# The second cross attention of a two-layer decoder, by half token tiles with folded keys

## The reference

```python
def _L1_xattn_ref(inputs_q, inputs_kv, Wq, Wk, Wv, Wo, bo, gq, gk):
    ...
    q = jnp.einsum('bsd,dhe->bshe', inputs_q, Wq)
    k = jnp.einsum('bsd,dhe->bshe', inputs_kv, Wk)
    v = jnp.einsum('bsd,dhe->bshe', inputs_kv, Wv)
    q = _rmsnorm(q, gq)
    k = _rmsnorm(k, gk)
    head_dim = q.shape[-1]
    scores = jnp.einsum('bqhe,bkhe->bhqk', q, k) / jnp.sqrt(jnp.asarray(head_dim, q.dtype))
    attn = jax.nn.softmax(scores, axis=-1)
    x = jnp.einsum('bhqk,bkhe->bqhe', attn, v)
    out = jnp.einsum('bqhe,hed->bqd', x, Wo) + bo
    return out
```

## Time and profile before

| | us |
|---|---|
| median of three runs | 1205.21 |
| lowest and highest | 1202.03, 1206.45 |
| profiled execution, its own time | 1207.17 |
| its span in the trace | 1205.5 |
| PE busy | 894.1 (74%) |
| DVE busy | 871.1 (72%) |
| ACT busy | 661.3 (55%) |
| POOL busy | 256.1 (21%) |

### The profile page before, as it was taken

One profiled execution on the slowest core, in us unless ns is written; L12 is line 12 of the kernel. 1 busy time (PEld: TensorE's weight loads), 2 busy tenths in 40 slices (PEclk: granted clock), 3 DMA queues, 4 the chain that ended last, 5 costly groups with the idle time before them and its releaser, 6 DMA issues. The chain is left out here.

```text
span 1205.5 us, 12085 instructions
## 1 busy us (share of the span) xinstructions
PE 894.1 (74%) x3656; PEld 499.5 (41%) x3656; DVE 871.1 (72%) x1703; ACT 661.3 (55%) x1829; POOL 256.1 (21%) x153
## 2 busy tenths in 40 slices
PE   2561478998989589898815248599898976898893
PEld 2450335554366334344414124455435643344432
DVE  1268646886389589999716875587846967999993
ACT  1413369992435285785712053999352435686691
POOL 1011106884070100000000200288515201000000
PEclk9865587998979799999957558699997997999997
DMA  8100012330000000000010000133100000000000
GB/s 217 35 0 1 0 40 59 93 94 0 1 1 1 1 0 1 0 1 1 1 50 1 0 1 5 58 97 90 35 1 1 1 1 1 1 0 1 1 0 18
DMA packets 26814, 27.41 MB, mean 23 GB/s; under 512 B 7172, under 2 KB 17146, under 8 KB 26746
## 3 DMA queue, kind: packets, MB, share of 16 engines
q1 hardware_dynamic: 24776, 24.63, 7.2%
q10 hardware_dynamic: 1970, 1.97, 0.6%
...
HBM read 25.28 MB, written 1.31 MB: 22 GB/s over the span
## 5 line engine op out<-in xcount | busy, mean ns | idle before, releaser
L1489 POOL TENSOR_TENSOR rs<-ve,minus_half 128x4 f32<-128x4 f32 (+2 forms) x60 | 101.7, 1702 | 816.0 <-DVE ve L1119 686.8
L877 PE MATMUL ps<-mem,ident 128*128 128x512 f32 x512 | 234.3, 607 | 27.7 <-DVE mem L1457 26.9
L909 ACT ACTIVATE mem<-ps 77x512 f32<-77x512 f32 (+7 forms) x172 | 103.6, 605 | 241.7 <-PE ps L818 61.1
L1079 ACT ACTIVATE mem<-mem 128x32 f32<-128x32 f32 x1024 | 217.8, 312 | 0.0
L1302 DVE TENSOR_TENSOR_SCAN mem<-mem,ps 128x1024 f32<-128x1024 f32 x64 | 146.0, 2285 | 45.2 <-PE ps L722 45.2
L1504 POOL TENSOR_TENSOR mem<-mem 128x1024 f32<-128x1024 f32 x64 | 150.8, 2360 | 116.7 <-DVE mem L1302 116.6
L1457 DVE SCALAR_TENSOR_TENSOR mem<-mem 128x1024 f32<-128x1024 f32 x128 | 159.2, 1279 | 13.3 <-ACT mem L1079 11.8
L877 PEld LDWEIGHTS ps<-mem,ident 128*128 128x128 f32 x512 | 95.3, 192 | 165.7 <-issue 95.3
L729 PE MATMUL ps<-mem,ident 128*128 128x512 f32 x256 | 121.7, 602 | 0.0
L1449 DVE TENSOR_TENSOR mem<-mem 128x1024 f32<-128x1024 f32 x96 | 113.0, 1218 | 0.3
L1008 ACT ACTIVATE mem<-mem 128x256 f32<-128x256 f32 x256 | 105.2, 493 | 0.1
...
## 6 DMA issues: line engine op xcount, KB each, us to landing
...
```

Of the source, the lines that this page charges most:

```text
L877: mm = pe.matmul(ps[:, j, :], ident[:], WH[s][:, h % WB, j * 512:(j + 1) * 512], start=(h == 0), stop=(h == PH - 1), skip_group_check=True)
L909: ins = nc.scalar.activation(to, of, ACT.Copy, **kw)
L1079: ins = nc.scalar.activation(SVA[s][:, n % 2, i * NK:(i + 1) * NK], sims[:, 1, h, :], ACT.Identity, bias=sims[:, 0, h, i:i + 1])
L1489: nc.gpsimd.tensor_tensor(RS[s][0:rows, i * n:(i + 1) * n], VE[s][0:rows, i * n:(i + 1) * n], minus_half[0:rows, 0:n], ALU.pow)\
```

## The change

The fifth sublayer is computed in another arrangement, and part of it moves.

- The keys' part becomes a generator `memory`, merged with the scan's by stage (`merged`): keys and their squares come at stage 5 + NS of the scan, ahead of the scan's output product at 6 + NS. The gains are still folded into the turned keys; the keys are then folded with Wq: `KW` holds for each head a 128 x 77 matrix, made from `a_qT` (Wq turned once in preparation) and the keys, so scores come from x directly. Values times Wo are laid out as ten chunks of 128 rows of the 16 x 77 = 1232 (head, context) pairs (`VW`); the shifted context for a chunk that crosses a head comes from `CTP`, the context with 128 zero columns at either side.
- Queries are only made for their mean squares: tokens on partitions, a tile of 128 tokens by 1024 features in two banks, squared by ScalarE, reduced by VectorE, power by GpSimd, once for each tile.
- The loop runs over eight units u: four token tiles by two halves of eight heads. Scores of a unit are two matmuls of 308 columns into banks 0 and 1. VectorE takes the maximum of each head and multiplies it by minus the root (`NM`). ScalarE reads the scores from PSUM and writes the exponential, one instruction for each head, with `RS` as scale, `NM` as bias and the sum over the row in `SM`. VectorE takes the reciprocal and multiplies the probabilities of the unit (128 x 616).
- The probabilities of a tile are turned in ten chunks, in groups of 4, 4 and 2 (one group after the first half of heads, two after the second), copied by VectorE, and multiplied with `VW`; the result has tokens on the partitions, in bank 3, and the residual reads it there.
- The `BLEND_LANES` branches go; both lanes took them before, so the scan's instructions are the same.

The diff, cut to what is added in these places; lines removed in `cross1` are those described above.

```diff
@@ -84,10 +84,16 @@
-GB = 3
+HC_COLS = H * C
+CK = -(-HC_COLS // P)
+GROUPS = [(0, 4), (4, 8), (8, CK)]
+GROUPS_OF = [GROUPS[0:1], GROUPS[1:3]]
+def chunk_rows(i):
+    return min(P, HC_COLS - i * P)
...
+pe.wait_ge(p_late, ALL_LATE)
+for j in range(HP):
+    mm = pe.transpose(PS[0][:, j // 4, (j % 4) * P:(j % 4 + 1) * P], a_q[:, j * P:(j + 1) * P],
                       ident[:])
...
+def merged(*runs):
+    stage = [next(r, None) for r in runs]
+    while any(n is not None for n in stage):
+        n, i = min((n, i) for i, n in enumerate(stage) if n is not None)
+        yield n
+        stage[i] = next(runs[i], None)
...
+def memory(s):
+    ps = PS[s]
+    yield 5 + NS
+    w.next(G("scan_done", s))
+    for j in range(2):
+        pe.matmul(ps[0:C, 2 + j, :], CTP[s][:, P:P + C], a_k[:, j * 512:(j + 1) * 512],
+                  start=True, stop=True).then_inc(G("k_ready", s), 1)
+    yield 5.9 + NS
+    w.next(G("kn_ready", s))
+    for j in range(HP):
+        mm = pe.transpose(ps[:, 2 + j // 4, (j % 4) * C:(j % 4 + 1) * C],
+                          KN[s][:, 2 * j:2 * j + 2, :].rearrange("p a b -> p (a b)"),
+                          ident[0:C, 0:C])
+    mm.then_inc(G("k_ready", s), 1)
+    for half in range(2):
+        yield 6.2 + 0.2 * half + NS
+        if half == 0:
+            w.next(G("kT_ready", s))
+        else:
+            w.next(G("m_sb", s))
+        for j in range(4 * half, 4 * half + 4):
+            for a in range(2):
+                mm = pe.matmul(ps[:, 2 + a, j % 4 * C:(j % 4 + 1) * C],
+                               a_qT[a * E:(a + 1) * E, j, :], KT[s][a * E:(a + 1) * E, j, :],
+                               start=True, stop=True)
+        mm.then_inc(G("k_ready", s), 1)
+    for n, (c0, c1) in enumerate(GROUPS):
+        yield 6.6 + 0.1 * n + NS
+        if n >= 1:
+            w.next(G("v_sb", s))
+        for i in range(c0, c1):
+            rows = chunk_rows(i)
+            heads = [h for h in range(H) if h * C < i * P + rows and (h + 1) * C > i * P]
+            for h in heads:
+                at = P + i * P - h * C
+                mm = pe.matmul(ps[0:rows, 1, (i - c0) * P:(i - c0 + 1) * P],
+                               CTP[s][:, at:at + rows], a_vo[:, h, :],
+                               start=(h == heads[0]), stop=(h == heads[-1]))
+        mm.then_inc(G("v_ready", s), 1)
+def scan_memory(s):
+    yield from merged(scan(s), memory(s))
...
+for k in range(NB):
+    yield 1 + k
+    if k == 0:
+        w.next(G("xT_ready", s))
+        w.next(G("v_sb", s))
+    elif k == 1:
+        w.next(G("m_sb", s))
+    else:
+        w.next(G("qsq_ready", s))
+    for j in range(2):
+        mm = pe.matmul(ps[:, k % 2 * 2 + j, :], XT[s][:, k * P:(k + 1) * P],
+                       a_q[:, j * 512:(j + 1) * 512], start=True, stop=True)
+    mm.then_inc(G("aq_ready", s), 1)
+def scores(u):
+    k, g = u // 2, u % 2
+    if u == 0:
+        w.next(G("qsq_ready", s), 2)
+    else:
+        w.next(G("p_ready", s))
+    for a in range(2):
+        h = 8 * g + 4 * a
+        mm = pe.matmul(ps[:, a, 0:4 * C], XT[s][:, k * P:(k + 1) * P],
+                       KW[s][:, h:h + 4, :].rearrange("p a b -> p (a b)"), start=True, stop=True)
     mm.then_inc(G("s_ready", s), 1)
+def weights_turned(k, c0, c1):
+    if (c0, c1) in (GROUPS_OF[0][0], GROUPS_OF[1][0]):
         w.next(G("pn_ready", s))
+    if k or c0:
+        pe.wait_ge(G("wT_ready", s), k * len(GROUPS) + GROUPS.index((c0, c1)))
+    p = SC[s][:, k % 2].rearrange("p a b -> p (a b)")
+    for i in range(c0, c1):
+        rows = chunk_rows(i)
+        mm = pe.transpose(ps[0:rows, 2, (i - c0) * P:(i - c0 + 1) * P],
+                          p[:, i * P:i * P + rows], ident[:])
+    mm.then_inc(G("wT_turned", s), 1)
+def attended(k, c0, c1):
+    n = k * len(GROUPS) + GROUPS.index((c0, c1))
+    pe.wait_ge(G("wT_ready", s), n + 1)
+    for i in range(c0, c1):
+        rows = chunk_rows(i)
+        mm = pe.matmul(ps[:, 3, k * P:(k + 1) * P], AT[s][0:rows, n % 3, i - c0, :],
+                       VW[s][0:rows, i, :], start=(i == 0), stop=(i == CK - 1))
+    mm.then_inc(G("at_used", s), 1)
+    return mm
+yield 10
 scores(0)
+due = None
+for u in range(2 * NB):
+    if u + 1 < 2 * NB:
+        yield 14 + 4 * u
+        scores(u + 1)
+    for n, (c0, c1) in enumerate(GROUPS_OF[u % 2]):
+        yield 15 + 4 * u + n
+        weights_turned(u // 2, c0, c1)
+        if due:
+            attended(*due)
+        due = (u // 2, c0, c1)
+yield 15.5 + 8 * NB
+attended(*due)
...
+def memory(s):
+    ps = PS[s]
+    yield 5.1 + NS
     for j in range(2):
         w.next(G("k_ready", s))
         nc.scalar.activation(KQ[s][:].rearrange("p a b -> p (a b)")[:, j * 512:(j + 1) * 512],
+                             ps[0:C, 2 + j, :], ACT.Square).then_inc(G("ksq_ready", s), 1)
+    yield 6 + NS
+    w.next(G("k_ready", s))
+    copy(KT[s][:].rearrange("p (a b) c -> p a (b c)", a=2), ps[:, 2:4, 0:4 * C],
+         G("kT_ready", s), scale=a_g[:, 0:1])
+    for half in range(2):
+        yield 6.3 + 0.2 * half + NS
+        w.next(G("k_ready", s))
+        copy(KW[s][:, 8 * half:8 * half + 8, :].rearrange("p (j a) c -> p a j c", a=2),
+             ps[:, 2:4, 0:4 * C].rearrange("p a (j c) -> p a j c", c=C), G("m_sb", s))
+    for n, (c0, c1) in enumerate(GROUPS):
+        yield 6.65 + 0.1 * n + NS
         w.next(G("v_ready", s))
+        copy(VW[s][:, c0:c1, :].rearrange("p a b -> p (a b)"), ps[:, 1, 0:(c1 - c0) * P],
+             G("v_sb", s))
...
+for k in range(NB):
+    yield 1.5 + k
+    w.next(G("aq_ready", s))
+    if k >= 2:
+        w.next(G("ssq_done", s))
+    nc.scalar.activation(QSQ[s][:, k % 2].rearrange("p (a b) c -> p a (b c)", a=2),
+                         ps[:, k % 2 * 2:k % 2 * 2 + 2, :], ACT.Square)\
         .then_inc(G("qsq_ready", s), 1)
+def exponentials(u):
+    k, g = u // 2, u % 2
+    if k >= 2 and g == 0:
+        act.wait_ge(G("wT_turned", s), (k - 1) * len(GROUPS))
     w.next(G("l_ready", s))
+    for i in range(8):
+        h = 8 * g + i
+        ins = nc.scalar.activation(SC[s][:, k % 2, h, :],
+                                   ps[:, i // 4, i % 4 * C:(i % 4 + 1) * C], ACT.Exp,
+                                   scale=RS[s][:, k * H + h:k * H + h + 1],
+                                   bias=NM[s][:, i:i + 1], accum_out=SM[s][:, u % 2, i:i + 1])
+    ins.then_inc(G("p_ready", s), 1)
+for u in range(2 * NB):
+    yield 12 + 4 * u
+    exponentials(u)
...
+kv = VE[s][0:C, 64 - H:64]
+yield 5.3 + NS
 w.next(G("ksq_ready", s), 2)
+w.link(nc.vector.tensor_reduce(kv, KQ[s][:], AX.X, ALU.add))
+nc.vector.tensor_scalar(kv, kv, 1.0 / E, 1e-6, ALU.mult, ALU.add).then_inc(G("kvar_ready", s), 1)
+yield 5.8 + NS
+w.next(G("krstd_ready", s))
 w.next(G("k_ready", s), 2)
 for j in range(2):
     ins = nc.vector.tensor_tensor(
+        KN[s][:, j * 8:(j + 1) * 8, :], ps[0:C, 2 + j, :].rearrange("p (a b) -> p a b", b=E),
+        spread(RS[s][0:C, 64 - H + j * 8:64 - H + (j + 1) * 8], 2, E), ALU.mult)
 ins.then_inc(G("kn_ready", s), 1)
...
+for k in range(NB):
+    yield 1.7 + k
+    qv = VE[s][:, k * H:(k + 1) * H]
+    w.next(G("qsq_ready", s))
+    nc.vector.tensor_reduce(qv, QSQ[s][:, k % 2], AX.X, ALU.add).then_inc(G("ssq_done", s), 1)
+    w.next(G("ssq_done", s))
+    nc.vector.tensor_scalar(qv, qv, 1.0 / E, 1e-6, ALU.mult, ALU.add)\
+        .then_inc(G("var_ready", s), 1)
+def maxima(u):
+    k, g = u // 2, u % 2
     w.next(G("s_ready", s))
+    if g == 0:
         w.next(G("rstd_ready", s))
+    w.link(nc.vector.tensor_reduce(
+        MX[s][:], ps[:, 0:2, 0:4 * C].rearrange("p a (i c) -> p a i c", c=C), AX.X, ALU.max))
+    nc.vector.scalar_tensor_tensor(out=NM[s][:], in0=MX[s][:], scalar=-1.0,
+                                   in1=RS[s][:, k * H + 8 * g:k * H + 8 * g + 8],
+                                   op0=ALU.mult, op1=ALU.mult).then_inc(G("l_ready", s), 1)
+def weights(k, c0, c1):
+    n = k * len(GROUPS) + GROUPS.index((c0, c1))
+    w.next(G("wT_turned", s))
+    if n >= 3:
+        w.next(G("at_used", s))
+    nc.vector.tensor_copy(AT[s][:, n % 3, 0:c1 - c0, :].rearrange("p a b -> p (a b)"),
+                          ps[:, 2, 0:(c1 - c0) * P]).then_inc(G("wT_ready", s), 1)
+yield 11
+maxima(0)
+for u in range(2 * NB):
+    yield 13 + 4 * u
     w.next(G("p_ready", s))
+    nc.vector.reciprocal(RD[s][:, u % 2], SM[s][:, u % 2]).then_inc(G("rd_ready", s), 1)
+    yield 13.1 + 4 * u
+    w.next(G("rd_ready", s))
+    p = SC[s][:, u // 2 % 2, u % 2 * 8:u % 2 * 8 + 8, :]
+    nc.vector.tensor_tensor(p, p, spread(RD[s][:, u % 2], 2, C), ALU.mult)\
+        .then_inc(G("pn_ready", s), 1)
+    if u + 1 < 2 * NB:
+        yield 15 + 4 * u
+        maxima(u + 1)
+    for n, (c0, c1) in enumerate(GROUPS_OF[u % 2]):
+        yield 15.5 + 4 * u + n
+        weights(u // 2, c0, c1)
+yield 60
+dve.wait_ge(G("at_used", s), len(GROUPS) * NB)
+residual(s, bank(s, 3), a_bo)
...
+yield 305.4 + NS
+w.next(sg["kvar_ready"][s])
```

(12 more changed lines are left out.)

332 lines of the change are left out of this document (73 added, 259 removed).

## The result

The changed kernel takes 1220.4 us in the median (1216.9 to 1222.9, four runs); the kernel before took 1204.2 on the same chip. The ratio is 1.0127, 95% interval 1.0102 to 1.0152: slower by 12 to 18 us, where the prediction had said 32. The sign and the mechanism came out as forecast, the size at half.

The account below looks back on a forecast made before the run. Taken as bounds: TensorE in the stage's query half, VectorE in its loop. Steps sum to 136.1 against 124.6 us, +11.5 a pass, +15.5 with clock; 2 x 15.5 + 0.8 = +32, median 1237 us, range 1222 to 1252.

Parts of the forecast that it names:

- Keys first: Behind the scan's last accumulation: key matmuls, powers and turning delay the scan's output matmuls L749; 12.9 us.
- Output, fold, values: Ahead of turning x: scan output, folded keys and values in one row on TensorE; 21.0 us.
- Queries: Ahead of the loop: turning x, query matmuls, the last tile's mean squares and first maximum; 19.0 us.
- Clock, +3 in the prologue: Ahead of the loop: TensorE's clock falls after idling behind the keys; 3 us a pass, plus 1 in the tail.
- The loop: Second cross attention: eight rounds of both lanes at 9.8 us, less the last gap; 75.7 us a pass.
- e: In the loop: time of one group of eight exponentials on ScalarE at 0.44 us each; 3.55 us.
- a gap ended by L1373: In each loop round: ScalarE idles 2.7 us until VectorE, after both lanes' products, finishes lane 0's maximum and scale.
- Tail: After the loop: last products, then chunks turned, copied and summed up to the first residual; 7.5 us.
- Once, +0.8: In the preparation: turning a_q puts eight transposes before the last matmuls; +0.8 us, once.
- hidden read-out: Rival, loop: the sum's read-out overlaps the next exponential, so one costs 0.33 us; 1208 us, chance 0.14.
- sagging clock: Rival, loop: TensorE's clock falls to half and TensorE becomes the bound, +16 us a pass; 1269 us, chance 0.12.

Follow-up runs that it names:

- e3: Changed kernel with the values made right behind the scan's output matmuls, ahead of the keys' turning and fold; 1200.7 us, ratio 0.9953 to the kernel before.
- e5: Changed kernel with exponentials that don't sum (no accum_out), VectorE summing the block ahead of each reciprocal; 1212.1 us, ratio 1.0070 to the kernel before.
- e6: Changed kernel with the exponentials' scale operand replaced by the number 0.0625, of use for time only; 1200.7 us, ratio 0.9961 to the kernel before.
- e2: Changed kernel with lane 1's loop steps half a round behind lane 0's on VectorE and TensorE; 1178.3 us, ratio 0.9771 to the kernel before.
- e4: Changed kernel with the edits of e2 and e3 together; 1159.7 us, ratio 0.9601 to the kernel before.

## Why the prediction was right in sign and wrong in size

The step that failed is the loop's: an exponential was priced at 0.44 us and takes 0.39, which is 6.1 of the 8.8 us a pass by which the forecast was too high. The other 2.7 are durations ahead of the loop, most of them of matmuls, each taken a little too long.

The forecast was +15.5 us a pass, the trace shows +6.6 in pass one and +6.1 in pass two. Its steps, in pass one:

- **Keys first.** Right: L749 13.2 us behind the last accumulation, 12.9 forecast without and 15.9 with the allowance for the clock. e3 shows that the idle time there was real, and that nothing in the algorithm asked for it.
- **Output, fold, values.** Right: 21.3 us (293.94 to 315.24), 21.0 forecast. Two errors cancel. The values take 11.48 for 100 records, 0.115 each, where I had taken 0.13 from a group of 16; the output at the lower clock takes 6.21 instead of the 4.1 I had, which at full clock is 3.73 by e3.
- **Queries.** Right: 18.75 against 19.0.
- **Clock, +3 in the prologue.** By e3 this was there, and of the size forecast: the output takes 2.5 us less when TensorE has no gap, and of the turning of the keys about 0.5 was on the path (lane 1's; lane 0's ends ahead of the second idle time). But the first exponential came 53.2 us behind the zero, where 52.9 stood without the allowance and 55.9 with it. What was mis-sized are the durations beside it: values 1.5 us too long, output 0.5, fold, queries and the keys' part 0.25 each. Their sum nearly cancels the clock, and that the total without it comes out is luck. 2.7 us a pass.
- **The loop.** The term that was mis-sized. Its shape is right to the last instruction: groups of eight, a gap ended by L1373 (2.56 idle, or 2.7 as the forecast counted it, the round less two groups), VectorE half idle. But an exponential was put at 0.44 us and takes 0.39, so e is 3.15 and not 3.55, the round 9.04 and not 9.8, and the loop 69.6 us (333.99 to 403.6) and not 75.7. 6.1 us a pass. By e5 the 0.39 is made of 0.30 with both operands (0.33 forecast, from 0.36 less 0.03) and 0.09 for the read-out. The forecast had 0.11 for it, a difference that was put together from instructions of 512 and 616 columns; the earlier trace rows shows the 0.09 itself, as the distance from the read-out at 114.05 to the next instruction at 114.14. The second operand costs 0.09 by e6. Two pieces, each 0.02 to 0.03 too large, stand in front of 128 exponentials a pass.
- **Tail.** 8.4 us against 7.5 + 1: right.
- **Once, +0.8.** Not to be seen: the first turning of x lies at 44.9 us before and at 44.45 after, and at 42.5 to 46.2 in the experiments. It is below what one profiled execution differs from another.

-2.7 and -6.1 make -8.8, and with the tail's -0.1 that is what lies between 15.5 and 6.6. Of the rivals none happened as such. The hidden read-out had the distance at 0.33 and the time at 1208. The distance of 0.39 lies halfway between it and the forecast, and so does the time, but by e5 not for its reason: the read-out costs nearly what was forecast, and without it the distance is 0.30. A sagging clock is in the trace (0.79 in the loop) but not on the path: ScalarE waits for VectorE's L1373 in every round, and VectorE waits for scores only once in 334 to 400, for 0.3 us. It does lengthen the tail: four records of L837 took 1.11 there and 0.66 in the tail of e2. The Trainium skill (TensorE: Matmul & The Clock Gate, HAM oscillation) describes a loop whose idle gaps bring the clock down again and again; the trace agrees as to the clock, with 0.79 over 334 to 404 against 1.00 over 300 to 330, and the cost in the loop was nothing as long as TensorE had 9 us for its work.

What the prediction lacked was not a step but a question. It named the order on VectorE and the order on TensorE as the two costs and took both as part of the change. Both are a handful of stage numbers, and e4 shows that without them the same reorganisation is 4.0% faster than the kernel before.
